# Value products of four heads in the four column quarters of TensorE, and three shared-expert tiles moved behind the expert blocks

## The reference

```python
x = x + tanh(g_xattn[0]) * L0_xattn(ctx, layernorm(x), mask)      # 8 heads, 77 keys
x = x + tanh(g_ffn[0])   * L0_ffn(layernorm(x))                   # 64 experts, top 8, and a shared expert
x = x + tanh(g_xattn[1]) * L1_xattn(layernorm(x), ctx)            # 16 heads, 77 + 256 keys
x = x + tanh(g_ffn[1])   * L1_ffn(layernorm(x))                   # 8 experts with low-rank parts, top 2
```

## Time and profile before

| | |
|---|---|
| timed runs | 1472.48 us median of 3 (1469.11 to 1472.70) |
| span of the profiled execution, first to last instruction | 1466.6 us |
| median of the timed runs less that span | 5.9 us |
| mean granted TensorE clock | 0.969 |
| PE busy | 1334.5 us, 91% |
| DVE, ACT, POOL busy | 56%, 48%, 36% |
| second attention, eight batches | from 755.5 to 1146.6 us |

### The profile page before, as it was taken

How to read it: one execution, slowest core, us unless ns; L and a number is a source line. 1 busy time by engine, 2 the same in 40 slices (tenths; PEclk the granted TensorE clock), 3 DMA queues, 4 the chain that set the end, 5 groups by cost and what they waited for, 6 DMA issues and landing times. The chain is left out here.

```text
span 1466.6 us, 30458 instructions
## 1 busy us (share of the span) xinstructions
PE 1334.5 (91%) x8152; PEld 1054.1 (72%) x8152; DVE 823.1 (56%) x2153; ACT 709.9 (48%) x1871; POOL 528.0 (36%) x589
## 2 busy tenths in 40 slices
PE   5999899999999999999167899999998899999998
PEld 4886667777777777777054677676765789999997
DVE  7979814333333333333346577676768576666666
ACT  2444644444444444444043787777866444444443
POOL 1003353333333333331666666776451110111110
PEclk9999999999999999999568999999999999999999
DMA  4023116677576657642432121222110000000000
GB/s 108 0 88 94 40 46 189 210 218 222 160 216 178 176 161 222 191 120 91 133 111 84 47 63 59 58 58 62 51 67 16 23 15 15 9 7 14 15 8 15
DMA packets 105407, 134.03 MB, mean 91 GB/s; under 512 B 29587, under 2 KB 89331, under 8 KB 105299
## 3 DMA queue, kind: packets, MB, share of 16 engines
q1 hardware_dynamic: 62339, 59.05, 13.7%
q0 software_dynamic: 15456, 48.62, 12.0%
q10 hardware_dynamic: 27504, 25.05, 5.0%
HBM read 100.66 MB, written 32.01 MB: 90 GB/s over the span
## 5 line engine op out<-in xcount | busy, mean ns | idle before, releaser
L741 POOL DMA_INDIRECT xg<-n_rows,idx x191 | 181.2, 949 | 296.5 <-DVE wS L2105 220.4
L1242 PE MATMUL ps<-wgu,xT 128*128 x764 | 259.1, 462 | 0.3 <-ACT xT L1061 0.3
L1242 PE MATMUL ps<-wdn,hT 88*128 (+1 forms) x892 | 227.9, 380 | 2.4 <-ACT hT L1019 1.8
L2264 DVE TENSOR_REDUCE nmx<-ps 128x1 f32<-128x333 f32 x256 | 127.3, 498 | 118.6 <-PE ps L1242 96.7
L1120 ACT ACTIVATE pD<-ps,nmx 128x333 f32<-128x333 f32 x256 | 139.2, 546 | 98.1 <-DVE nmx L2264 74.1
L1242 PEld LDWEIGHTS ps<-wdn,hT 88*128 88x128 f32 x892 | 154.3, 190 | 20.6 <-issue 5.2
L2108 DVE TENSOR_TENSOR hC<-sg,ps 128x176 f32<-128x176 f32 x191 | 64.5, 338 | 172.9 <-ACT sg L1071 144.7
L1242 PEld LDWEIGHTS ps<-wgu,xT 128*128 128x128 f32 x764 | 130.0, 190 | 41.7 <-issue 0.8
L771 POOL DMA_INDIRECT yg<-y_rows,slotG x128 | 123.5, 965 | 88.2 <-issue 36.2
L2111 DVE COPY hT<-ps 88x256 f32<-88x256 f32 x191 | 80.3, 421 | 132.6 <-issue 82.9
L1552 PE MATMUL ps<-ident,pD 128*128 128x128 f32 x768 | 130.8, 281 | 23.9 <-DVE pT L2270 15.2
(11 more groups left out here) (306 smaller groups left out, 2996.5 us busy)
## 6 DMA issues: line engine op xcount, KB each, us to landing
y_rows<-yC ACTq DMA_DIRECT2D x191, 128.0 KB
wgu<-in_wgu SPq DMA_DIRECT2D x64, 352.0 KB
wdn<-in_wdn SPq DMA_DIRECT2D x64, 176.0 KB
xg<-n_rows,idx POOLq DMA_INDIRECT x191
kraw<-in_kD SPq DMA_DIRECT2D x8, 308.0 KB
x<-in_x SPq DMA_DIRECT2D x4, 512.0 KB, 4.5
n_rows<-nB SPq DMA_DIRECT2D x4, 512.0 KB, 4.3
yg<-y_rows,slotG POOLq DMA_INDIRECT x128
```

What stands on the lines that cost most here:

```text
L741: pool.indirect_dma_start(out=xg[:, b % XS, :], out_offset=None, in_=n1_rows, in_offset=bass.IndirectOffsetOnAxis(ap=idx[:, b:b + 1], axis ...
L1242: return pe.matmul(o, lhsT, rhs, start=start, stop=stop, **kw)
L2264: dve.tensor_reduce(nmx[:, k:k + 1], ps[:, score_bank(k), 0:NK1], AX, ALU.max, negate=True).then_inc(d_mx, 1)
```

## The change

Heads are put in an order in which four neighbours lie in four quarters, and `d_values` is called for four heads at steps 1, 9, 17 and 25. `pT` has five slots, given out by a table. Of the shared tiles, 13 run where all 16 ran and three (`NLATE`) behind block 191, with their turned rows kept in `nTL`; DVE multiplies and adds for these. POOL issues its first four gathers ahead of tile 12, and starts batch 1's gathers only when the late tiles are added. SP's raw loads wait for the late tiles' gate-and-up products. Some small buffers change their place in memory.

```diff
 HG1 = 8
-HPV = 2
+HPV = 4
 HQ = P // 32
-ORDER = [4 * g + h for g in range(H1 // 4) for h in (0, 2, 1, 3)]
+ORDER = [8 * g + 2 * q + e for g in range(H1 // 8) for e in range(2) for q in range(HQ)]
+PT_SLOTS = 5
+PT_SLOT = (0, 1, 2, 3, 4, 0, 2, 3, 1, 0, 3, 4, 2, 1, 3, 4)
 NG1 = H1 // HG1
...
 NSH = 2
+NLATE = 3
+NEARLY = NT - NLATE
 WSLOT = 8
...
             pD = s("pD", [P, AHEAD, NK1])
-            pT = s("pT", [P, 2 * HPV, 3, SEQ])
             den = s("den", [P, NG1, HG1, TB])
...
             attN = s("attN", [P, NG1, SEQ])
+            pT = s("pT", [P, PT_SLOTS, 3, SEQ])
             size_d = free0 - nc.sbuf_bytes_remaining
...
         VALUES_AFTER = 2
+        ROWS_NEEDED_AT = (0, 4, 16, 20)
         SCORE_BANKS = (0, 1, 7)
+
+        def pT_before(n):
+
+            same = [m for m in range(n) if PT_SLOT[m] == PT_SLOT[n]]
+            return same[-1] if same else max(m for m in range(H1) if PT_SLOT[m] == PT_SLOT[n]) - H1
...
             is_q = 1 - (j - U_ROWS) % 2
-            return 1 - is_q if j >= UNITS - 2 else is_q, 2 * ((j - U_ROWS) // 2)
+            return 1 - is_q if j >= UNITS - 4 else is_q, 2 * ((j - U_ROWS) // 2)
...
+            load_keys(0)
+            sp.wait_ge(l_gu, 2 * NLATE)
             load_raw(0)
             load_raw(1)
-            load_keys(0)
             sp.wait_ge(d_zero, ZERO_PIECES)
...
             pool.wait_ge(b_rwd, 16)
-            for t in range(TABLED_AT, NT):
+            pool.wait_ge(b_er, 1)
+            pool.wait_ge(b_idx, 1)
+            for b in range(XS // 2):
+                gather(b)
+            for t in range(TABLED_AT, NEARLY):
                 s_step(t, t % 2, t // 2)
-                if t == TABLED_AT:
-                    pool.wait_ge(b_er, 1)
-                    pool.wait_ge(b_idx, 1)
-                for b in range(2 * (t - TABLED_AT), 2 * (t - TABLED_AT) + 2):
-                    gather(b)
-            for b in range(2 * (NT - TABLED_AT), XS):
+            for b in range(XS // 2, XS):
                 gather(b)
-            s_sum(NT - 1, (NT - 1) % 2)
+            s_sum(NEARLY - 1, (NEARLY - 1) % 2)
             for b in range(XS, NRUN):
...
             gather_y(0, 0)
+            pool.wait_ge(l_x, NLATE)
             for k in range(FIRST_GATHERS):
...
-            act.wait_ge(s_gu, 2 * NT)
+            act.wait_ge(s_gu, 2 * NEARLY)
             c_copy_xT(0, 0)
-            s_copy_hT(NT - 1)
-            act.wait_ge(s_h, 2 * NT)
-            s_y_out(NT - 1, 1, NT // 2 - 1)
+            s_copy_hT(NEARLY - 1)
+            act.wait_ge(s_h, 2 * NEARLY)
+            s_y_out(NEARLY - 1, (NEARLY - 1) % 2, (NEARLY - 1) // 2)
             blocks(act, c_step, extra=2)
+
+            def l_copy_hT(n):
+                act.wait_ge(l_th, n + 1)
+                if n == 0:
+                    act.wait_ge(c_dn, NEARLY + NRUN)
+                after(act, l_dn, n)
+                act.copy(hT[:], ps[0:IC, 5, :].rearrange("p (f c n) -> p f c n", f=2, c=2)).then_inc(l_hT, 1)
+
+            def l_step(n):
+                for f in range(2):
+                    act.wait_ge(l_gu, 2 * n + f + 1)
+                    if n == 0:
+                        act.wait_ge(c_h, NRUN)
+                    after(act, l_h, 2 * n + f - 1)
+                    act.activation(sg[:, f, :], ps[:, 2 + f, 0:I0], ACT.Silu).then_inc(l_silu, 1)
+                if n:
+                    l_copy_hT(n - 1)
+
+            for n in range(NLATE):
+                l_step(n)
+            l_copy_hT(NLATE - 1)
...
                 act.wait_ge(d_pt, STEPS * b + k + 1)
-                after(act, d_pv, H1 * b + h - 2 * HPV + 1)
-                act.copy(pT[:, h % (2 * HPV), :, t * P:(t + 1) * P], ps[:, 5 + k % 2, 0:3 * P].rearrange("p (c n) -> p c n", c=3)).then_inc(d_eva, 1)
+                after(act, d_pv, H1 * b + pT_before(h) + 1)
+                act.copy(pT[:, PT_SLOT[h], :, t * P:(t + 1) * P], ps[:, 5 + k % 2, 0:3 * P].rearrange("p (c n) -> p c n", c=3)).then_inc(d_eva, 1)
...
-            for t in range(TABLED_AT, NT - 1):
+            for t in range(TABLED_AT, NEARLY - 1):
                 s_step(t, t % 2, t // 2)
...
             pe.wait_ge(b_idx, 1)
             for j in range(2):
                 load_slot(j)
-            s_step(NT - 1, (NT - 1) % 2, NT // 2 - 1)
+            last_early = NEARLY - 1
+            s_step(last_early, last_early % 2, last_early // 2)
             c_transpose(0)
-            s_transpose_h(NT - 1)
-            pe.wait_ge(s_u, 2 * NT)
-            pe.wait_ge(s_silu, 2 * NT)
+            s_transpose_h(last_early)
+            pe.wait_ge(s_u, 2 * NEARLY)
+            pe.wait_ge(s_silu, 2 * NEARLY)
             c_up(0)
-            s_down(NT - 1, (NT - 1) % 2)
-            pe.wait_ge(s_hT, NT)
-            pe.wait_ge(s_y, NT)
+            s_down(last_early, last_early % 2)
+            pe.wait_ge(s_hT, NEARLY)
+            pe.wait_ge(s_y, NEARLY)
             for j in range(NRUN + 1):
                 c_step(j)
+
+            def l_up(n, f):
+                if n == 0:
+                    pe.wait_ge(c_h, NRUN)
+                after(pe, l_h, 2 * n + f - 1)
+                for c in range(DC):
+                    last = mm(ps[:, 2 + f, 0:GU], turned(NEARLY + n)[:, c, :], wgu[:, f, c, :], c == 0, c == DC - 1)
+                last.then_inc(l_gu, 1)
+
+            def l_transpose_h(n):
+                pe.wait_ge(l_h, 2 * n + 2)
+                if n == 0:
+                    pe.wait_ge(c_hT, NRUN)
+                after(pe, l_hT, n)
+                for f in range(2):
+                    last = transpose_h(f, 5, 2 * P * f)
+                last.then_inc(l_th, 1)
+
+            def l_down(n):
+                pe.wait_ge(l_hT, n + 1)
+                if n == 0:
+                    pe.wait_ge(c_y, NRUN)
+                after(pe, l_x, n - 1)
+                for f in range(2):
+                    for c in range(2):
+                        last = mm(ps[:, 6 + n % 2, 0:D], hT[:, f, c, :], wdn[:, f, c, :], f == 0 and c == 0, f == 1 and c == 1)
+                last.then_inc(l_dn, 1)
+
+            for n in range(NLATE):
+                l_up(n, 0)
+                if n:
+                    l_transpose_h(n - 1)
+                l_up(n, 1)
+                if n:
+                    l_down(n - 1)
+            l_transpose_h(NLATE - 1)
+            l_down(NLATE - 1)
+            pe.wait_ge(l_x, NLATE)
...
                 h, t = head_of(k), k % TB
-                if k % (TB * 4) == 0:
-                    pe.wait_ge(d_ea, UNITS * b + U_ROWS + 2 * (k // (TB * 4)) + 2)
+                if k in ROWS_NEEDED_AT:
+                    pe.wait_ge(d_ea, UNITS * b + U_ROWS + 2 * ROWS_NEEDED_AT.index(k) + 2)
                 if k == 0:
...
                         at = 32 * (h // 2 % HQ)
-                        last = mm(ps[at:at + 32, 4, 0:SEQ], v1[0:rows, s, c, h // 2, 2 * (h % 2):2 * (h % 2) + 2, :].rearrange("p a d -> p (a d)"), pT[0:rows, n % (2 * HPV), c, :],
+                        last = mm(ps[at:at + 32, 4, 0:SEQ], v1[0:rows, s, c, h // 2, 2 * (h % 2):2 * (h % 2) + 2, :].rearrange("p a d -> p (a d)"), pT[0:rows, PT_SLOT[n], c, :],
                                   c == 0 and h % 2 == 0, c == 2 and h % 2 == 1, skip_group_check=True)
...
                 dve.wait_ge(d_pt, STEPS * b + k + 1)
-                after(dve, d_pv, H1 * b + h - 2 * HPV + 1)
-                dve.tensor_copy(pT[:, h % (2 * HPV), :, t * P:(t + 1) * P], ps[:, 5 + k % 2, 0:3 * P].rearrange("p (c n) -> p c n", c=3)).then_inc(d_evd, 1)
+                after(dve, d_pv, H1 * b + pT_before(h) + 1)
+                dve.tensor_copy(pT[:, PT_SLOT[h], :, t * P:(t + 1) * P], ps[:, 5 + k % 2, 0:3 * P].rearrange("p (c n) -> p c n", c=3)).then_inc(d_evd, 1)
...
             dve.memset(ps[:, 4, 0:SEQ], 0.0).then_inc(d_zero, 1)
-            dve.wait_ge(s_add, NT)
+            dve.wait_ge(s_add, NEARLY)
+
+            def l_sum(n):
+                t = NEARLY + n
+                dve.wait_ge(l_dn, n + 1)
+                dve.scalar_tensor_tensor(out=x[:, t:t + 1, :], in0=ps[:, 6 + n % 2, None, 0:D], scalar=tg[:, 2:3],
+                                         in1=x[:, t:t + 1, :], op0=ALU.mult, op1=ALU.add).then_inc(l_x, 1)
+
+            for n in range(NLATE):
+                for f in range(2):
+                    dve.wait_ge(l_silu, 2 * n + f + 1)
+                    if n == 0:
+                        dve.wait_ge(c_th, NRUN)
+                    after(dve, l_th, n)
+                    dve.tensor_tensor(hC[:, f, :], sg[:, f, :], ps[:, 2 + f, I0:GU], ALU.mult).then_inc(l_h, 1)
+                if n:
+                    l_sum(n - 1)
+            l_sum(NLATE - 1)
+            dve.wait_ge(l_x, NLATE)
...
                 begin()
```

More of the change, by code:

```diff
@@ L126, in bass_flamingo @@
         nS = sb("nS", [P, 2, D])
-        nT = sb("nT", [P, 2, DC, P])
         nTs = sb("nTs", [P, DC, SEQ])
         lg = sb("lg", [P, NT, E1])
-        idx = sb("idx", [P, NBLK], I32)
-        slot_row = sb("slot_row", [1, NBLK], I32)
```

(31 more changed lines are left out.)

## The result

| | before | after |
|---|---|---|
| median of 4 runs, us | 1470.8 (1466.4 to 1472.7) | 1456.4 (1453.8 to 1457.8) |
| ratio | | 0.9911, 95% interval 0.9897 to 0.9926 |
| span of the profiled execution, us | 1466.6 | 1453.1 |

The account below looks back on a forecast made before the run. TensorE (PE), busy 91% of the span, was taken as the leading bound, though not alone in the attention. Gains of 25 us (attention) and 11 (early tiles), late tiles costing 0, turn 1472.5 us into about 1436; range 1419 to 1460.

Parts of the forecast that it names:

- Four quarters at once: Second attention's value products: a four-head call costs about 1.42 us, so 32 of 64 calls, 45.4 us of PE, fall away.
- Shared tiles leave early, 11.0 us: Ahead of the expert blocks: moving tiles 13, 14 and 15 away gains 11.0 us (bounds 8 and 13.9).
- Cost 0 (up to 3 if a tile takes 5.5 us): Behind the last expert block: three late tiles, 16.5 us of work, fit PE's 32.26 us gap at no cost.
- the 721 forecast: Start of the second attention: its first `nS` transposes were to come near 721 us, against 732.13 before.
- POOL's 16 gathers as cover: Behind the last block: late tiles finish 6.7 us ahead of batch 0's 16 gathers (20 us), so POOL's new wait is free.
- 25 us (bounds 0 and 45.4): Second attention, all eight batches: the part of the 45.4 us saved on PE that reaches the end.
- 3.3 us a batch, 20 us: Attention batches 1 to 6: gain of 2.1 us in steps 0 to 15 and 1.2 in steps 16 to 31.
- DVE wait for POOL's `ysum`: Attention batches, near step 15: DVE would come 2.84 us earlier for POOL's sum and wait 1.6 us, about half hidden.
- Batch 0, "2.5 us": First batch of the second attention: gain 2.5 us, though PE is idle 18 of its 67.5 us.
- Batch 7, "2.5 us": Last batch of the second attention: gain 2.5 us, with DVE busy as much as 79%.

Follow-up runs that it names:

- e11: Changed kernel with VectorE's two small variance operations moved from step 12 to step 15; 1420.4 us, where the kernel before took 1452.2.
- e7: Changed kernel with GpSimd's first 16 gathers of expert rows held until the last late sum is done; 1462.2 us.
- e8: Changed kernel with two late shared tiles instead of three; 1451.6 us.
- e3: Changed kernel with SyncE's loads of raw weights, values and keys behind the last late sum instead of behind the late up products; 1456.1 us.
- e6: Changed kernel with nine filler products on TensorE behind the last late transposes and the last late down product; 1458.1 us.
- e5: Changed kernel with GpSimd's 128 indirect gathers replaced by plain transfers of consecutive rows of the same size; 1415.5 us.
- e16: Changed kernel with VectorE's two small variance operations at step 15 instead of 12, on the fourth chip; 1449.9 us.
- e13: Changed kernel as it is, beside the kernel before on a fourth chip; 1456.6 us against 1470.6.
- e9: Kernel before with its 128 gathers replaced by plain transfers of consecutive rows of the same size; 1442.4 us.
- e15: Judging by the order of the runs: kernel before with the four-quarter value products alone, repeated on a fourth chip; 1458.1 us.
- e2: Kernel before with the four-quarter value products alone; 1457.1 us.

## Why the prediction fell short, step by step

**Four quarters at once: right.** A call of four heads was costed at 1.42 us and takes 1.43.

**Shared tiles leave early, 11.0 us: right.** The last block's down product starts at 687.29, 11.45 us earlier.

**Late tiles, "Cost 0 (up to 3 if a tile takes 5.5 us)": wrong, 7.0 us.** This is one of two steps that failed. The tiles do take 5.7 us each (694.46 to 700.14) and not 4.53, and that alone is covered: in e11, on the chip without late completions, they cost 1.5 us or less, and the attention's first transposes are at 722.15, 10.0 us earlier than in the earlier trace rows and 1 us from the 721 forecast. On the other chips the completions of the last two tiles come late beside the gathers, by 3.6 and 6.0 us in the changed kernel's trace. I took POOL's 16 gathers as cover; there they are what delays the work under it. e7 (gathers away, hold gone) and e8 (two tiles, ahead of the hold) show it; e3 rules out SyncE's loads, and e6 speaks against the rival that only the last thing PE does is late.

**"25 us (bounds 0 and 45.4)" for the attention: 10.4 measured.** This is the other. Its terms:
- Batches 1 to 6, "3.3 us a batch, 20 us": 12.0 measured. The step that failed is what I put in the way of PE. I had DVE wait for POOL's `ysum`; no such wait exists in the changed kernel, nor in e5 or e11. In its place PE waits for DVE's copies of `pT`, 16.8 us instead of 3.8, and 13.7 of that stays in e11. That is what PE meets first when its own work shrinks. What I had at nothing are the holds, and DVE's operation of 1.55 us beside POOL's add, which makes the `pT` copy behind it late. PE is idle 33 us of the six batches, 18 before and 25 in e11, which has neither. In the trace of before the same operation is as slow in two of batches 1 to 4, 1.48 us at 981.28, but a call of `d_values` that starts at 981.95 covers it, one of those that the change removes; a stall lost its cover. That is the question I asked of my own edits and not of the kernel's existing stalls. With the operation moved and no hold (e11) the six batches take 255.3 us, 24.4 less than in the earlier trace rows's trace of the kernel before (another chip) and more than the 20 forecast. With plain transfers they gain 22.1 (274.4 less 252.3). That both come near 20 doesn't confirm my split: it had a wait in it that isn't there. Of the 12 us between 267.7 and 255.3 the shares of the operation and of the holds are not separated (batch 1 has only holds, batches 2 to 4 have both); in e16, with holds left and the operation moved, the six take 258.1 us (e13: 268.2).
- Batch 0, "2.5 us": 2.0 lost. Even with plain transfers it gains nothing (57.3 and 57.9). I had written that PE is idle 18 of its 67.5 us and still gave it a share. Much of that idle time is holds: the batch takes 69.5 us in the changed kernel, 70.2 in e16, which has the operation moved and the holds, and 57.8 in e11, which has no hold.
- Batch 7, "2.5 us": 0.4 measured, 0.4 with plain transfers. DVE is busy 80% of it and PE 77%; no run tests what bounds it.

The sum, measured: 5.0 us at the first scores (755.5 to 750.5) and 10.4 in the batches, less 1.9 us that the stage behind them took longer, which is within what it varies between profiled executions of these kernels (319.9 to 322 us): 13.5 of span. So the measured time lies in the stated range, and that is not because the account was right: the value products' call and the early tiles were, the cover and the wait behind POOL were not.

Two pairs tell what the change is worth without late completions: 27 us with plain transfers (e9, e5), and about 32 with the moved operation where the holds are absent (1452.2 to 1420.4 in e11). The changed kernel as it is did not run on that chip.

**What stays open.** Why PE's completions come late beside a row of indirect gathers, and why on four chips of five and not on the fifth, isn't settled. Each chip was used in one job, so chip and job aren't told apart. One rival is untested: the profiler's own records. Where completions are late, the trace also lacks semaphore updates. Up to 680 us the changed kernel's has 649 of the 919 that PE's instructions make, e11's on the fifth chip 916 of 917; from 680 to 1130 us it has 765 of 806, e5's 837 of 837. Every timed run is on record with a span and a clock, so none here shows the kernel without such records. Gathers and record writing may get in each other's way, and the holds may be smaller, or absent, in a run without them. Nor is it settled whether plain transfers cure it by being shorter on POOL or by not gathering.

## What to carry to other kernels

Before another engine's idle time is used as cover, look at what runs in it: cover and disturbance can be the same instructions. Waits that the profile ascribes to nobody ("remote") in the trace of before are a price that the moved work may meet; here ACT and DVE had 15 of them between 680 and 1130 us, 36 us in all, 22 of it in batch 0, and I did not read them. And when a stage gets faster, look for short operations that were slow and hidden; ask what is under the piece that goes away.

## What the hardware showed unexpectedly

- Beside a row of GpSimd's indirect gathers, TensorE's completions reached ScalarE and VectorE late on four chips, by 6 us in the changed kernel and at most by 11.6 (e15). On a fifth chip, and with plain transfers of the same size, none was over 0.2 us late between 680 and 1130 us. For the kernel before the chips give 1468 to 1471 against 1452 us; whether all of that is late completions no run shows, and whether the profiler's records have a part in it is open.
- Plain transfers from GpSimd's queue cost it 0.54 us each (16 in 8.60 us), the indirect ones 1.25.
- An operation of VectorE on 128x2 elements took 0.17 us alone and mostly 1.3 to 1.6 us beside GpSimd's adds (2.3 and 2.4 us once each, in e2 and e3).
- Four column quarters, each with a product of two records for each key chunk, ran 24 records in the time of 12 (1.43 and 1.42 us).
